# Layer-3 storage order, load times, finish order and table load in a four-layer kernel

## The chip, the cores and the metric

One NeuronCore of a Trainium2 chip. The metric is device time in microseconds of one execution; the number shown is the median of three runs.

## What is computed

x has 4 sequences of 256 tokens by 256 channels, 1024 tokens. Four layers are added in turn, x = x + ffn_l(cond_l(...)). Each cond_l is a gated two-sided recurrence over the tokens (a "ratio" of two scans) times a sigmoid of x. The feed-forward parts differ:

- layer 0: ternary weights and int8 activations (256 to 1024 to 256);
- layer 1: a mixture of 8 experts, two per token, exact gelu, f32 weights;
- layer 2: int weights with zero point 128, silu(gate) * up, 256 to 704 (stored as 768) to 256;
- layer 3: layer norm, then two linear maps in MXINT8, 256 to 1024 to 256, with a tanh gelu between. Both operands are quantised in blocks of 32 along the contraction:

```python
def mx_quant(x):                 # blocks of 32 along the last axis
    amax = max(abs(block)); scale = 2 ** (floor(log2(amax)) - 6)
    return clip(round(block / scale), -128, 127) * scale
h = mx_layernorm(x, ln_w, ln_b)
h = mx_gelu(bf16(mx_quant(h) @ mx_quant(W1).T + b1))
out = bf16(x + bf16(mx_quant(h) @ mx_quant(W2).T + b2))
```

The order in which the 1024 inner units of layer 3 stand in memory is free, as long as blocks of 32 stay blocks.

## The kernel before

It is written with five hand-ordered instruction streams (SP, POOL = GpSimd, ACT = ScalarE, DVE = VectorE, PE = TensorE) and semaphores; every order below is written out in the code, and each engine works in order.

**Expert loop (L950 DVE, L1250 PE, L570 ACT).** 24 tiles of 128 token slots. In iteration j PE multiplies tile j by its expert's first matrix (L1259), transposes tile j+1 (x_transpose), multiplies tile j-1 by the second matrix (down_tile, L1243), and transposes tile j's hidden values (L1269). DVE adds the bias (L954), does one piece of side work, copies the output of tile j-1 to yo (L226) and half of hT (L978). ACT does gelu (L581), the other half of hT (L587), the copy of the transposed input (copy_xT, L544), the store of yo and the load of xg three tiles ahead. The side work of DVE: the recurrences of layers 2 and 3 in j < 18 (ratio_step; the last ratio is ready at j = 17); the absolute maxima and clipping of the third layer's weights W1 and W2 in j = 19 to 22 (L964, block_scales L937, L967); the conversion of layer 2's integers in j = 23 (L971, L973). ACT issues the loads: load_w3 at j = 18 behind the last ratio (L553), load_rows at 19 (L566), load_l2 at 20 (L561).

**The inner index.** Inner unit h of layer 3 is 32n + j (n the block). Before, it is stored j-major, 32 blocks to a run. So W1 is loaded in four transfers of permuted rows of 1 KB (L555 to L557), b1 in three transfers of single 4-byte elements by SP (L283), W2's quantised form is written turned by POOL (L402 to L404), and the gelu's quantiser takes its maxima over a view whose inner step is 32 elements (L1065); the products with `inverse` and `unit` (L1075, L1080) repeat a run of 32. The bias rows br sit in partitions 0, 64 and 96 of brf, which POOL clears (L386) and splits into three bf16 parts (L388 to L392); the matmul with `pick` (L1346, L1364) adds them. POOL then quantises W1 and W2 (L399 to L404) and PE transposes them behind the loop (transpose_w3, L233), into banks 0 to 3.

**Between the layers.** PE transposes the ratio of layer 3 into banks 3 to 6 (L1276), then adds the experts' bias part for all tokens into banks 0 to 3 (L1283). DVE adds all four banks to x (L993), then runs combine(0), scale_y2T(0), combine(1) (L1090). combine(p) needs the two gathered expert rows of each token of group p, which POOL fetches by indirect DMA (L414), after the gather of cb (L410).

**Groups (L1093 DVE, L1368 PE, L646 ACT).** Layers 2 and 3 run over G = 4 groups of two tiles, in rounds p = 0 to 5: layer 2 of group p beside layer 3 of group p-1 and p-2. Layer 2: x_to_channels (L1296), sigmoid_l2, scale_y2T, six chunks of gate_up_l2 (L1309, silu_l2 L613, gate_l2 L1012) in three banks that rotate by the list `turns`, down_l2 (L1318), add_l2 (L1018). Layer 3: norm_stats, norm_apply, norm_quant, norm_to_channels (L1332), copy_hqT (L618), up_l3 (L1344, L1346), gelu_l3 (L625 twice, L630), gelu_scales (L1065 to L1069), gelu_quant (L1075 to L1080), turn_l3 (L1355), copy_q3T, down_l3 (L1363), copy_ob (L643), finish_tile (L1086, L1087), and SP's store. On DVE a round runs: add_l2, finish_tile, norm_stats, scale_y2T, gates with the norm's steps between them, finish_tile, gelu_scales and gelu_quant of tile 2p-3, gelu_scales and gelu_quant of tile 2p-2, combine(p+2).

## Time and profile before

| | us |
|---|---|
| median of 3 runs | 616.39 (616.28 to 618.4) |
| profiled execution, own time | 620.55 |
| its span | 618.5 |
| PE busy / DVE busy | 376.3 / 429.3 |
| ACT busy / POOL busy | 229.8 / 180.1 |

The granted clock of TensorE was 0.83 of full speed on average. A timeline row gives start, duration, engine, line, operation, and in brackets how long the engine was idle before it and who released it. "PEld" is a weight load, "ACTq" and "SPq" are DMA issues. A row may merge neighbours ("x16"); its duration is then their stretch.

### The profile page before, as it was taken

The numbers are of one execution on the slowest core, as the hardware profiler recorded it, in microseconds if no ns is written. First come the engines' busy times: TensorE is split into PE (matmuls) and PEld (weight loads), VectorE is DVE, ScalarE is ACT, GpSimd is POOL, SyncE is SP. The second block draws the span as 40 slices with busy tenths as digits, with TensorE's granted clock in tenths as the row PEclk, the third lists the DMA queues.
The fourth block names the chain that finished last, engine by engine and source line by source line (L and its number), as shares of the span: only waits on it lengthen the run. The fifth ranks groups of instructions, "written<-read, shape, count | busy, mean of one in ns | idle before, by whom it ended". The sixth has DMA issues, their size and how long they took to land.

```text
span 618.5 us, 5497 instructions
## 1 busy us (share of the span) xinstructions
PE 376.3 (61%) x1680; PEld 259.5 (42%) x1680; DVE 429.3 (69%) x615; ACT 229.8 (37%) x333; POOL 180.1 (29%) x116
## 2 busy tenths in 40 slices
PE   0000260435454204999999999946948699798552
PEld 0000220213243102667767766624646577676421
DVE  5999759798774886856966867326673346789873
ACT  4626651447756121222222222202202236365451
POOL 4600213953003483440360330036364600000000
PEclk9999856575678555899999999987977699799875
DMA  8900000000027521281061561995001300000000
GB/s 296 333 0 0 1 0 0 1 0 0 0 98 246 210 76 47 91 302 38 27 205 35 196 212 34 45 153 179 17 10 51 93 1 0 1 10 17 10 17 17
DMA packets 34673, 47.46 MB, mean 77 GB/s; under 512 B 5699, under 2 KB 28758, under 8 KB 34646
## 3 DMA queue, kind: packets, MB, share of 16 engines
q1 hardware_dynamic: 23046, 31.76, 15.1%
q10 hardware_dynamic: 10032, 11.14, 8.2%
q0 software_dynamic: 1568, 4.20, 2.1%
q8 instruction: 15, 0.25, 0.2%
q14 instruction: 12, 0.10, 0.1%
HBM read 37.67 MB, written 9.44 MB: 76 GB/s over the span
## 4 chain that ended last, share of the span: by engine, by line
PE 42%; DVE 19%; issue 19%; POOL 7%; ACT 6%; DMA 6%; ACTq 1%; SPq 0%; POOLq 0%; DVEq 0%
PE bank L1259 12%; PE bank L1243 11%; PE bank L1309 6%; DMA ekv<-in_w3b 4%; POOL slot_rows L375 3%; PE bank L1269 3%; PE bank L1163 3%; DVE scr L723 2%; DVE small L1065 1%; PE bank L1283 1%; DMA small<-in_s_gu 1%; DVE scr L973 1%; POOL ekv L326 1%; PE bank L1318 1%; POOL scr L334 1%
## 5 line engine op out<-in xcount | busy, mean ns | idle before, releaser
L1243 PE MATMUL bank<-big,yT 128*128 x384 | 91.6, 394 | 16.8 <-ACT yT L587 16.8
L1259 PE MATMUL bank<-big,ygT 128*128 x192 | 90.5, 616 | 1.8 <-ACT ygT L544 1.1
L1243 PEld LDWEIGHTS bank<-big,yT 128*128 128x128 f32 x384 | 74.3, 198 | 28.3 <-issue 18.4
L954 DVE TENSOR_TENSOR yT<-bank,big 128x512 f32<-128x512 f32 x48 | 32.8, 689 | 42.7 <-PE bank L1259 42.7
L351 POOL TENSOR_TENSOR small<-small 128x2 f32<-128x2 f32 (+1 forms) x9 | 9.1, 1009 | 173.4 <-DVE small L1032 88.0
L587 ACT ACTIVATE yT<-bank 128x512 f32<-128x512 f32 x24 | 14.3, 597 | 109.3 <-DVE yo L226 82.7
L1259 PEld LDWEIGHTS bank<-big,ygT 128*128 128x128 f32 x192 | 36.0, 198 | 39.3 <-issue 39.3
L1309 PE MATMUL bank<-yT,scr 128*128 128x256 f32 x192 | 46.7, 403 | 0.0
L1163 PE MATMUL bank<-big 128*128 128x512 bf16 x64 | 22.6, 515 | 30.9 <-DVE big L828 29.9
L1309 PEld LDWEIGHTS bank<-yT,scr 128*128 128x128 f32 x192 | 38.6, 205 | 5.5
L340 POOL TENSOR_TENSOR scr<-scr 128x1024 f32<-128x1024 f32 x5 | 15.5, 3108 | 87.1 <-DVE scr L723 87.1
L544 ACT ACTIVATE ygT<-bank 128x256 f32<-128x256 f32 x24 | 9.2, 384 | 66.9 <-PE bank L1234 61.2
L1142 PE MATMUL bank<-identf,yT 128*128 128x128 f32 x16 | 3.6, 417 | 41.8 <-DVE yT L791 41.8
L581 ACT ACTIVATE yT<-yT 128x512 f32<-128x512 f32 x48 | 27.7, 622 | 3.1 <-DVE yT L954 3.1
L226 DVE COPY yo<-bank 128x256 f32<-128x256 f32 x24 | 10.0, 418 | 26.6 <-PE bank L1243 22.2
L331 POOL TENSOR_TENSOR g<-g,ek 128x1024 f32<-128x1024 f32 x8 | 19.0, 2372 | 28.7 <-ACT g L448 28.6
L1269 PE MATMUL bank<-identf,yT 128*128 128x128 f32 x192 | 25.6, 278 | 2.4 <-ACT yT L581 2.4
L1234 PE MATMUL bank<-identf,xg 128*128 128x128 f32 x48 | 9.7, 287 | 27.4 <-DMA xg<-slot_rows 27.4
L1163 PEld LDWEIGHTS bank<-big 128*128 128x128 bf16 x64 | 7.1, 120 | 44.2 <-DVE big L828 34.0
L1269 PEld LDWEIGHTS bank<-identf,yT 128*128 128x128 f32 x192 | 22.9, 143 | 5.0 <-ACT yT L581 2.7
L375 POOL DMA_INDIRECT slot_rows<-y,posi x16 | 20.6, 1289 | 12.6 <-DVE posi L907 8.0
L1234 PEld LDWEIGHTS bank<-identf,xg 128*128 128x128 f32 x48 | 6.8, 147 | 40.6 <-issue 33.8
(284 smaller groups left out, 891.7 us busy)
## 6 DMA issues: line engine op xcount, KB each, us to landing
big<-in_moe_w SPq DMA_DIRECT2D x16, 1024.0 KB, 7.0
big<-in_moe_b SPq DMA_DIRECT2D x8, 512.0 KB, 8.8
slot_rows<-zeros SPq DMA_DIRECT2D x1, 3072.0 KB, 12.9
xg<-slot_rows ACTq DMA_DIRECT2D x24, 128.0 KB, 2.1
slot_outputs<-yo ACTq DMA_DIRECT2D x24, 128.0 KB, 1.7
v<-in_kT SPq DMA_DIRECT2D x1, 1024.0 KB, 5.0
yT<-in_xT SPq DMA_DIRECT2D x1, 1024.0 KB, 8.1
big<-in_gateT SPq DMA_DIRECT2D x1, 1024.0 KB, 10.1
```

The source lines that it names most:

```text
L331: link(gp.tensor_tensor(g[:, l, k], g[:, l, k], ek[:, k], ALU.subtract))
L340: link(gp.tensor_tensor(den[n % 2], den[n % 2], db[:], ALU.add))
L375: gp.indirect_dma_start(out=XG, out_offset=bass.IndirectOffsetOnAxis(ap=posi[:, k, i:i + 1], axis=0), in_=y1[:, i], in_offset=None).then_i ...
L581: sc.activation(h1[:, h * 512:(h + 1) * 512], h1[:, h * 512:(h + 1) * 512], ACT.Gelu).then_inc(s["h1_ready"], 1)
L587: sc.activation(hT[:, 0:4], ps[5][:].rearrange("p (c t) -> p c t", c=4), ACT.Copy).then_inc(s["hT_copy"], 1)
L954: ve.tensor_tensor(h1[:, h * 512:(h + 1) * 512], ps[1 + 2 * (j % 2) + h][:], big[:, bass.ds(at + (B1_AT + h * 512), 512)], ALU.add).then_i ...
L1163: ins = te.matmul(ps[6 + m - 2 * (n % 2)][:], q0T[:, k, tile_cols(i)], wgu_t[:, m, k, h * 512:(h + 1) * 512], start=(k == 0), stop=(k == K ...
L1234: ins = te.transpose(ps[0][:, k * P:(k + 1) * P], xg[:, j % 3, k * P:(k + 1) * P], identf[:])
L1243: ins = te.matmul(ps[7][:, 0:C], hT[:, c], big[:, bass.ds(at + (W2_AT + c * C), C)], start=(c == 0), stop=(c == IC - 1))
L1259: ins = te.matmul(ps[1 + 2 * (j % 2) + h][:], ygT[:, j % 2, k], big[:, bass.ds(at + (k * HI + h * 512), 512)], start=(k == 0), stop=(k == ...
L1269: ins = te.transpose(ps[5 + h][:, (c % 4) * P:(c % 4 + 1) * P], h1[:, c * P:(c + 1) * P], identf[:])
L1309: ins = te.matmul(bank_of((p, c))[:, m * 256:(m + 1) * 256], qgu[:, m, k, c * P:(c + 1) * P], yT[:, k, 256 * p:256 * (p + 1)], start=(k == ...
```

## The change

- **Inner index.** Unit h = 8i + r (i in 0 to 127, r in 0 to 7) is now stored r-major: eight runs of 128. A block of 32 is then 4 neighbours in each of the 8 runs. W1 is loaded in one transfer with 8 KB in a row per partition; W2 is quantised in plain order and read by transpose_w3 with a step of 8 elements; b1 is read by L1346 with a step of 8. The maxima go over two axes with runs of 4; `inverse` and `unit` are written four times each, 128 wide.
- **Bias rows.** No POOL clear and no SP transfers: both rows are broadcast to all partitions with the other rows by ACT (5 transfers), at j = 18, behind the last ratio.
- **Load times.** load_w3 at j = 15 (waiting for the scans and the products with v), load_rows at 18, load_l2 at 19.
- **Entry.** The experts' bias goes to banks 3, 4, 5 and 7; each combine(p) adds its own. Group 0's chunks come ahead of group 1's transposes, sigmoid and scaling, on PE, ACT and DVE.
- **Finishes.** finish_tile of tiles 5, 6 and 7 stands behind gelu_quant of tile 7.
- **Table.** The gelu table load stands ahead of copy_hqT.

```diff
-        turns = ["x0", "x1"]
+        turns = ["x0"]
         for p in range(G):
-            turns += [(p, c) for c in range(HC2)] + ([f"x{p + 2}"] if p + 2 < G else [])
+            turns += [(p, c) for c in range(HC2)]
+            if p == 0:
+                turns += ["x1", "x2"]
+            elif p + 2 < G:
+                turns += [f"x{p + 2}"]
+        bias_banks = (3, 4, 5, 7)
...
-            pe.wait_ge(s["w3q"], 2 * KC)
+            pe.wait_ge(s["w3q"], 2)
...
-                        src = w3q[:, 1, k * H3 + c * P:k * H3 + (c + 1) * P]
+                        src = w3q[:, 1, k * H3:(k + 1) * H3].rearrange("p (i r) -> p r i", r=HC3)[:, c]
...
-            sp.wait_ge(s["br_zero"], 1)
-            for row in (0, 64, 96):
-                sp.dma_start(brf[row:row + 1, 0:H3].rearrange("p (j n) -> p j n", n=32),
-                             A["b3a"].rearrange("(n j) -> j n", n=32).unsqueeze(0),
-                             allow_slow_non_contiguous=True).then_inc(s["ld_bias"], 16)
-                sp.dma_start(brf[row:row + 1, H3:H3 + C], A["b3b"].unsqueeze(0)).then_inc(s["ld_bias"], 16)
...
-            pool.wait_ge(s["ratio_ready"], 2 * L)
-            gp.memset(brf, 0.0).then_inc(s["br_zero"], 1)
-            pool.wait_ge(s["ld_bias"], 16 * 6)
+            pool.wait_ge(s["ld_l3rows"], 16 * 5)
...
-                for k in range(KC):
-                    n = slice(32 * k, 32 * (k + 1))
-                    turned = w3q[:, m, k * H3:(k + 1) * H3].rearrange("p (j n) -> p n j", n=32) if m else \
-                        w3q[:, m, k * H3:(k + 1) * H3].rearrange("p (n j) -> p n j", j=32)
-                    gp.tensor_tensor(turned, w3v[:, n], half[:, n], ALU.subtract).then_inc(s["w3q"], 1)
+                gp.tensor_tensor(w3q[:, m].rearrange("p (n j) -> p n j", j=32), w3v, half, ALU.subtract).then_inc(s["w3q"], 1)
...
             def load_w3():
-                act.wait_ge(s["ratio_ready"], 2 * L)
-                rows = A["w3a"].rearrange("(n c j) k -> j n c k", n=32, c=HC3)
-                for j in range(4):
-                    act.dma_start(w3nat[0][32 * j:32 * (j + 1)].rearrange("p (c k) -> p c k", c=HC3), rows[j]).then_inc(s["ld_w3"], 16)
+                act.wait_ge(s["scanned"], 2 * len(POOL_SUMS))
+                act.wait_ge(s["gv_ready"], 2 * L)
+                act.dma_start(w3nat[0].rearrange("p (c k) -> p c k", c=HC3),
+                              A["w3a"].rearrange("(p c) k -> p c k", c=HC3)).then_inc(s["ld_w3"], 16)
...
             def load_rows():
-                for dst, n in ((sdrow, "s_down"), (lnw, "ln_w"), (lnb, "ln_b")):
+                act.wait_ge(s["ratio_ready"], 2 * L)
+                for dst, n in ((sdrow, "s_down"), (lnw, "ln_w"), (lnb, "ln_b"), (brf[:, 0:H3], "b3a"), (brf[:, H3:H3 + C], "b3b")):
...
             for j in range(TILES):
-                if j == 18:
+                if j == 15:
                     load_w3()
+                elif j == 18:
+                    load_rows()
                 elif j == 19:
-                    load_rows()
-                elif j == 20:
                     load_l2()
...
-                if p + 1 < G:
+                if p >= 1 and p + 1 < G:
                     sigmoid_l2(p + 1)
...
+                if p == 0:
+                    sigmoid_l2(1)
                 if 1 <= p <= G:
+                    sc.preload_act_table(ACT.Gelu_apprx_tanh)
                     copy_hqT(p - 1)
                     gelu_l3(2 * p - 2)
...
-            for p in range(G):
+            def combine(p):
                 dve.wait_ge(s["bias_ready"], p + 1)
-                ve.tensor_tensor(pair(x, p), pair(x, p), ps[p][:], ALU.add).then_inc(s["bias_added"], 1)
-
-            def combine(p):
+                ve.tensor_tensor(pair(x, p), pair(x, p), ps[bias_banks[p]][:], ALU.add).then_inc(s["bias_added"], 1)
...
-            unit = ex3[:, 1].bitcast(BF16)[:, 0:32]
-            inverse = ex3[:, 2].bitcast(BF16)[:, 0:32]
+            unit = ex3[:, 1:3].rearrange("p m n -> p (m n)").bitcast(BF16)[:, 0:P]
+            inverse = ex3[:, 1:3].rearrange("p m n -> p (m n)").bitcast(BF16)[:, P:2 * P]
...
-                link(ve.tensor_reduce(top3, gl3[i % 2].rearrange("p (j n) -> p n j", n=32), AX.X, ALU.max, apply_absolute_value=True))
+                link(ve.tensor_reduce(top3, gl3[i % 2].rearrange("p (r n q) -> p n r q", r=HC3, q=4), AX.XY, ALU.max, apply_absolute_value=True))
...
             combine(0)
             scale_y2T(0)
-            combine(1)
             for p in range(G + 2):
                 if 1 <= p <= G:
                     add_l2(p - 1)
-                if p >= 3:
+                if 3 <= p <= G:
                     finish_tile(2 * p - 5)
...
-                if p + 1 < G:
+                if p >= 1 and p + 1 < G:
                     scale_y2T(p + 1)
                 if p < G:
                     gate_l2(p, 0)
+                if p == 0:
+                    combine(1)
...
+                if 2 <= p <= G:
+                    finish_tile(2 * p - 4)
                 if p >= 2:
-                    finish_tile(2 * p - 4)
                     gelu_scales(2 * p - 3)
...
+                if p == 0:
+                    scale_y2T(1)
                 if p + 2 < G:
                     combine(p + 2)
-            finish_tile(T - 1)
+            for i in range(T - 3, T):
+                finish_tile(i)
...
+            pe.wait_ge(s["r3_copy"], 2)
+            pe.wait_ge(s["r3_copy2"], 2)
...
-                    te.matmul(ps[4 + h][:], pick[:], br[:, h * 512:(h + 1) * 512], start=False, stop=True).then_inc(s["u3_ready"], 1)
+                    te.matmul(ps[4 + h][:], pick[:], br[:, 0:H3].rearrange("p (i r) -> p r i", r=HC3)[:, 4 * h:4 * h + 4], start=False, stop=True).then_inc(s["u3_ready"], 1)
...
-                if p + 1 < G:
+                if p >= 1 and p + 1 < G:
                     x_to_channels(p + 1)
...
+                if p == 0:
+                    x_to_channels(1)
                 if p < G:
                     down_l2(p, 0)
```

## Rows read from the trace of the kernel before

**Rows 1.** The timeline around expert tile 19 (start us, us, engine, line, what; idle before)

```profile
403.91 1.04 PE L1269 MATMUL bank<-identf,yT 128*128 128x128 f32 x8
...
413.97 2.29 DVE L964 TENSOR_REDUCE small<-ek 128x64 f32<-128x2048 f32 x1 [12.73 <-DMA ekv<-in_w3b]
...
427.71 1.04 PE L1269 MATMUL bank<-identf,yT 128*128 128x128 f32 x8
...
435.69 1.04 PE L1269 MATMUL bank<-identf,yT 128*128 128x128 f32 x8
```

**Rows 2.** The timeline where VectorE works beside GpSimd

```profile
417.11 2.65 DVE L941 TENSOR_SCALAR small<-small 128x64 f32<-128x64 f32 x1
...
447.00 10.83 POOL L404 TENSOR_TENSOR v<-ekv,tcmp 128x1024 bf16<-128x1024 f32 x2
...
448.90 4.43 DVE L971 TENSOR_SCALAR scr<-scr 128x3072 f32<-128x3072 int32 x1
...
453.25 5.69 DVE L973 SCALAR_TENSOR_TENSOR scr<-scr 128x1536 f32<-128x1536 int32 x1
...
460.42 6.74 PE L1243 MATMUL bank<-big,yT 128*128 x16 [7.94 <-ACT yT L587]
```

**Rows 3.** The timeline of groups 1 to 3

```profile
516.91 0.59 ACT L618 ACTIVATE big<-bank 128x512 bf16<-128x512 bf16 x1
...
519.68 1.28 ACT L630 ACT_TABLE_LOAD   x1
...
529.08 1.11 PE L1296 MATMUL bank<-identf,x 128*128 128x128 f32 x4 [3.58 <-DVE x L1000]
...
529.98 3.62 PE L1309 MATMUL bank<-yT,scr 128*128 128x256 f32 x8
...
547.12 2.86 PE L1318 MATMUL bank<-scr,big 128*128 128x256 f32 x12 [0.23 <-DVE big L1012]
...
570.71 2.86 PE L1318 MATMUL bank<-scr,big 128*128 128x256 f32 x12 [0.71 <-DVE big L1012]
```

**Rows 4.** The timeline of the tail, tiles 6 and 7

```profile
595.26 1.88 DVE L1065 TENSOR_REDUCE small<-big 128x32 f32<-128x1024 bf16 x1 [1.40 <-ACT big L630]
...
605.87 1.86 DVE L1065 TENSOR_REDUCE small<-big 128x32 f32<-128x1024 bf16 x1
...
610.15 0.69 DVE L1080 TENSOR_TENSOR big<-big,small 128x1024 bf16<-128x1024 bf16 x1
...
616.00 0.42 DVE L1087 TENSOR_TENSOR x<-x,big 128x256 f32<-128x256 f32 x1
```

**Rows 5.** The DMA issues (KB each, us from issue to landing)

```profile
ekv<-in_w3b ACTq DMA_DIRECT2D x1, 1024.0 KB, 22.6
...
cb<-slot_outputs,crow_i POOLq DMA_INDIRECT x1, 2.2
```

**Rows 6.** Groups by form from 380 us on (busy us, mean ns of one)

```profile
L1065 DVE TENSOR_REDUCE small<-big 128x32 f32<-128x1024 bf16 x8 | 15.0, 1877 | 7.0 <-ACT big L630 6.8
...
L404 POOL TENSOR_TENSOR v<-ekv,tcmp 128x1024 bf16<-128x1024 f32 x2 | 10.8, 5612 | 0.1
...
L404 POOL TENSOR_TENSOR v<-ek,small 128x1024 bf16<-128x1024 f32 x2 | 3.8, 1912 | 0.1
...
L1045 DVE TENSOR_REDUCE small<-big 128x16 f32<-128x512 bf16 x4 | 2.7, 679 | 0.0
```

**Rows 7.** The chain that ended last, group 1 and 2 (start us, us, what)

```profile
518.16 0.22 PE bank L1346
...
537.47 6.92 PE bank L1309 x32
```

**Rows 8.** The timeline at the entry of layer 2

```profile
472.56 6.37 PE L1283 MATMUL bank<-cb,big 16*128 16x256 f32 x16 [1.87 <-DMA cb<-slot_outputs,crow_i]
...
475.33 0.96 POOL L414 DMA_INDIRECT g<-slot_outputs,posi  x1 [0.30 <-issue]
...
486.88 12.30 PE L1309 MATMUL bank<-yT,scr 128*128 128x256 f32 x48
```

More of the change, by code:

```diff
@@ L961, in _ @@
                     if j == 19:
-                        dve.wait_ge(s["ld_w3"], 80)
+                        dve.wait_ge(s["ld_w3"], 32)
                     if j % 2:
@@ L1064, in gelu_scales @@
                 top3 = ex3[:, 0, 0:32]
[L1065 removed]
+                link(ve.tensor_reduce(top3, gl3[i % 2].rearrange("p (r n q) -> p n r q", r=HC3, q=4), AX.XY, ALU.max, apply_absolute_value=True))
                 link(ve.tensor_scalar(top3.bitcast(I32), top3.bitcast(I32), 0x7F800000, None, ALU.bitwise_and))
                 link(ve.tensor_scalar(top3, top3, 2.0 ** -120, None, ALU.max))
[L1068 to L1069 removed]
+                bits = top3.bitcast(I32).unsqueeze(2).to_broadcast(by_block)
+                ve.tensor_scalar(inverse.bitcast(I16).rearrange("p (n q) -> p n q", q=4), bits, -1.0 / 65536, 260.0 * 128, ALU.mult, ALU.add)
+                link(ve.tensor_scalar(unit.bitcast(I16).rearrange("p (n q) -> p n q", q=4), bits, 1.0 / 65536, -6.0 * 128, ALU.mult, ALU.add))
             def gelu_quant(i):
[L1072 removed]
                 t = m3[:, 0:512].bitcast(BF16)
[L1074 to L1075 removed]
+                t3 = t.rearrange("p (r i) -> p r i", r=HC3)
+                g3 = gl3[i % 2].rearrange("p (r i) -> p r i", r=HC3)
+                link(ve.tensor_tensor(t3, g3, inverse.unsqueeze(1).to_broadcast([P, HC3, P]), ALU.mult))
                 link(ve.tensor_scalar(t, t, MAGIC, MAGIC, ALU.add, ALU.subtract))
@@ L1079, in gelu_quant @@
                     dve.wait_ge(s["q3_tr"], i - 1)
-                ve.tensor_tensor(q3[i % 2].rearrange("p (j n) -> p j n", n=32), t.rearrange("p (j n) -> p j n", n=32),
-                                 unit.unsqueeze(1).to_broadcast(by_block), ALU.mult).then_inc(s["q3_ready"], 1)
+                ve.tensor_tensor(q3[i % 2].rearrange("p (r i) -> p r i", r=HC3), t3,
+                                 unit.unsqueeze(1).to_broadcast([P, HC3, P]), ALU.mult).then_inc(s["q3_ready"], 1)
                 dve.wait_ge(s["q3_ready"], i + 1)
@@ L1282, in _ @@
             for i in range(T):
-                ins = te.matmul(ps[i // 2][:, (i % 2) * C:(i % 2 + 1) * C], gcT[:, tile_cols(i)], cb[:], start=True, stop=True)
+                ins = te.matmul(ps[bias_banks[i // 2]][:, (i % 2) * C:(i % 2 + 1) * C], gcT[:, tile_cols(i)], cb[:], start=True, stop=True)
                 if i % 2:
@@ L1288, in x_to_channels @@
                 pe.wait_ge(s["l1_done"], 2 * p + 2)
-                if p == 0:
-                    pe.wait_ge(s["bias_added"], G)
                 if freed(f"x{p}"):
@@ L1326, in norm_to_channels @@
                     pe.wait_ge(s["q3T_ready"], 2 * p - 1)
-                else:
-                    pe.wait_ge(s["r3_copy"], 2)
-                    pe.wait_ge(s["r3_copy2"], 2)
                 for k in range(KC):
@@ L1361, in down_l3 @@
                     pe.wait_ge(s["ob_ready"], i)
+                else:
+                    pe.wait_ge(s["bias_added"], G)
                 for c in range(HC3):
```

10 lines of the change are left out of this document (3 added, 7 removed).

## The prediction, made before the run

> **What bounds the kernel now.** I read the page first, for the stages, then the timeline from 388 us on, because the change touches nothing before expert tile 15 and the first stall that it can reach is at tile 19. The expert loop is paced by TensorE at 7.98 us a tile: the transposes of two neighbouring tiles start at 427.71 and 435.69 [rows 1]. One interval is 23.80 us, from 403.91 to 427.71. In it VectorE's first reduction of the third-layer weights sits 12.73 us on the load of ekv until 413.97 [rows 1], and its copy of hT, for which TensorE waits, is queued behind it. In the last tile VectorE converts weights beside GpSimd: L971 and L973 together hold it from 448.90 to 458.94, and TensorE's L1243 starts at 460.42 after 7.94 us of idleness [rows 2]. The third and fourth layers then run as groups of two tiles. In group 1 TensorE is idle 3.58 us before L1296, for combine(3) on VectorE; in groups 2 and 3 it runs nearly without a gap, with 0.23 and 0.71 us at L1318 [rows 3]. From 595 us on the kernel is one serial chain of gelu, quantiser, transposes, product and finish, tile after tile [rows 4].
>
> **The weight load (gain 14.8).** It is issued at tile 15 instead of 18, three tiles or 24 us sooner, at about 365. Even with the 22.6 us to landing that it took [rows 5] it is there at 388, and tile 19 wants it near 400; its two transfers go past ACT's xg load, which is not wanted for nearly two tiles, and its new waits (scans and the products with v) end around tile 13. SP's six bias loads go. So 23.80 - 7.98 = 15.8 us come back. Against it: the five row broadcasts are issued at tile 18 (a few us of ScalarE's time, where it waits for TensorE's transposes of xg anyway), GpSimd's bias work (five operations) starts when they land, and VectorE's small operations of tile 19 meet it. L941, on 64 columns, took 2.65 us when GpSimd was busy [rows 2], and 64 columns are no work for that. Four such, with the hT copy behind them, cost 0 (bias work over in time) to 3; I take 1.0, as the copy has a few us of slack behind TensorE's L1259.
>
> **Tile 23 (gain 6.5).** GpSimd's last writes of w3q were turned, 5612 ns per 1024 columns against 1912 for plain ones [rows 6]. L971 ends some 1.6 us after the first turned write, L973 just after the second, at 457.83: they wait for GpSimd. With one plain write of 2 x 1.91 from 447.00 GpSimd ends at 450.8; L971 is done at 452.4, and L973 (1536 columns at L1045's 1.04 ns [rows 6] and a fixed part of 0.15: 1.75) at 454.2. Before, that was 458.94: 4.8, with the rounding of the copies behind it 5.0. Then the clock: L1243's 16 matmuls took 6.74 us here after the idle time and 3.46 is the price of 16 like ones at pace [rows 7]. With some 2.9 us of idleness (452.5 to 455.4) it may stay up or not, 0 to 3.1; I take 1.5. The turned third-layer weight is instead read by TensorE in steps of 16 bytes: 16 transposes, priced below, 0 to 2.5 (a quarter of 0.65 each), taken at 0.5 because the gather of cb hides the rest.
>
> **Entry of layer 2 (gain 5.4).** The first chunk of L1309 starts at 486.88, behind group 1's transposes, which wait for combine(1) [rows 8]. Bias banks 3, 4, 5 and 7 free VectorE of three bias additions ahead of combine(0). What limits combine(0) then is the gather of tile 1, issued at 475.33, landing 2.2 later by the cb gather's time [rows 5]: 477.5, and 1.0 for its two operations, 478.5. TensorE's bias products end at 478.9 [rows 8], so they are the next limit. Transposes (1.1, as at L1296 [rows 3]), sigmoid and scaling (each the size of L1045's 0.68) follow: first chunk at 481.5. combine(1), 2.7 us with its addition (0.68), goes between the first two gates, while a slow first chunk of 3.5 us leaves VectorE little else; group 1's transposes go into the gap before L1318, and its scaling and combine(2) are done within L1318's 24 products. I cost these at nothing; without that cover they would cost up to 2.7.
>
> **Groups 1 to 3 (cost 4.0, less 1.1).** ScalarE works in order, so the gelu load, 1.28 us, now starts after the group's last silu, and copy_hqT behind it. Before, that copy followed the silu at once (516.91) and the load came later, at 519.68 [rows 3]. For the gelu nothing changes: the load only moves ahead on the same chain. For TensorE, which waits for hqT, 1.28 us are new. Next, L1346 reads br with a step of 8 bf16. No row has TensorE reading so. Contiguous it takes 0.22 us in the chain [rows 7] at the high clock, the lower end; the upper end is VectorE's L1065, which at a 64-byte step needs (1877 - 150) / 1024 = 1.69 ns a column against 1.04 for L1045 [rows 6], so 0.86 us. I take a doubling, 0.43, nearer to TensorE's own row: plus 0.43 a tile on the gelu's chain, 0.86 a group on TensorE. The Trainium skill, "SBUF — State Buffer" (Door 1: the DMA port swizzle, the note on cachelines), says that full bandwidth needs two hits on each 16-byte line, and also that eight bf16 can be stridden for free. This step is exactly on that border: by the second half the price is nil and the sum 3 us better, by the first it is a penalty of unstated size. No run here shows it. On VectorE each quantiser gains: L1065 in runs of four costs about 1.22 us like L1045's rate (0.65 less), two small writes of 128 instead of 32 columns 0.1 more each: 0.45 net. Group 1: gelu 0.43 late, quantiser 0.45 faster, bias addition 0.68 more: 0.7 late for combine(3). Group 2 is bound by TensorE: 1.28 less 0.23 of idleness at L1318, plus 0.86: 1.9. Group 3: 1.28 less 0.71, plus 0.86: 1.4 [rows 3]. Together 4.0; with free reading 1.9, at the upper end 8.4. Group 1's gap of 3.58 us cost clock: eight matmuls of L1309 took 3.62 us behind it; 32 of them took 6.92 later, 1.73 for eight [rows 3, 7]. The gap shrinks to about 2; that gives back 0 to 2.2, taken 1.1.
>
> **Tail (gain 7.4).** Here ScalarE is idle before hqT, so the load is hidden: gelu(6), for which L1065 of tile 6 waited 1.40 us, comes 1.3 sooner, 0.4 less for L1346: L1065 at 594.3 instead of 595.26 [rows 4]. Scales and quantiser take 4.98 us (605.87 to L1080's end, 610.85), less 0.45: done at 598.85. L1065 of tile 7 follows at once instead of at 605.87, where it stood behind finish_tile(6) and so behind tile 6's product: done at 603.4 against 610.85. finish_tile(5), needed by the last copy_ob, and (6) run during tile 7's transposes and product, which take the old 5.57 us (610.85 to 616.42): end 609.0 instead of 616.42.
>
> **Sum.** 14.8 + 6.5 - 0.5 + 5.4 - 4.0 + 1.1 + 7.4 = 30.7 us. Against the profiled execution's 620.55 (span 618.5) this is 589.9; the runs' median is 616.39, 4.2 lower, so I forecast 585.7, told as 586.
>
> **Rivals.** (a) The 16-byte step costs TensorE nothing: 3.0 better, 582.7. For it: the step is a quarter of L1065's, the only slow read that the trace has. Against it: that row is over 1.6 times the contiguous price a column. Chance 0.22. (b) It costs the upper end, 0.65 us a matmul; 14 of 16 lie in the path, the 16 transposes count a quarter each, so 18 x 0.65 less 2.0 of slack, 9.7 instead of 3.0: 592.4. Chance 0.15. (c) The gelu load is hidden in groups 1 to 3 too, if the last silu leaves earlier than norm_to_channels ends: 3.6 better, 582. Against it: the copy at 516.91 follows its silu without a gap [rows 3]. Chance 0.06. (d) The gathers land late once the bias additions no longer cover them: half the entry's gain is lost, 588.5. Chance 0.05. (e) Slower than before: the strided read is priced as GpSimd's turned write, 5612 / 1024 = 5.5 ns a column [rows 6], 2.87 us a matmul. Then 18 x 2.66 less 2.0 is 45.9, against 33.7 of gains without that cost: 628.6. It decides from 2.2 us a matmul on, ten times the plain price. Against it: those writes were slowed by VectorE's work beside them. Chance 0.02. (f) The wait at tile 19 does not go, because the transfer's slowness is in the load itself: even then it lands ten us ahead of the need. Chance under 0.01. The forecast keeps 0.50.
>
> **Numbers.** The range 579.5 to 595 holds (a) to (d) with the unknown costs (clock 0 to 5.3, GpSimd beside VectorE 0 to 3, the strided price) and leaves out their coincidences and (e). Half a per cent, 3 us, is about what a measurement can tell from no change. Faster needs a gain of only 3 of 30.7: 0.97; within 0.5% 0.01; slower 0.02.
>
> **What would show it.** Right: transposes L1269 every 8 us through tiles 18 to 21; L973 under 2.5 us; the first chunk of L1309 before L1296 of group 1, about 5 us after group 0's; in groups 1 to 3 the table load ahead of L618, with TensorE idle over 2 us there; L1346 about 0.2 us longer; L1065 at 1.2; last L1065 about 4.6 us after the one before. Wrong: a VectorE wait on a load at tile 19, combine(0) waiting for gathers beyond 479, L1346 unchanged or 0.65 longer, or a last quantiser waiting for its gelu.

## The result, and the profile after

The changed kernel takes **597.83 us** (median of 4 runs, 595.41 to 600.27); the kernel before took 617.11 us beside it (4 runs, 616.28 to 618.4). The ratio is 0.969, with a 95% interval from 0.963 to 0.974. It is faster by 3.1%, some 19 us. The forecast was 586.0 us, with a range from 579.5 to 595: the sign was right, the gain was foreseen some 60% too large (30.7 us for 19.3), and the time lies above the range. The profiled execution took 595.98 us, with a span of 594.2.

A table by stage shows where the difference is. Its borders are starts of instructions that can be found in either timeline: the transposes of tiles 18 and 23 (L1269, now L1271), the four VectorE additions that end the groups (now L1013) and the last finish (now L1084). Line numbers have moved: L1243 is now L1245, L1309 L1311, L1318 L1320, L1346 L1345, L1065 L1061, L1087 L1084, L971 and L973 L968 and L970.

| Stage | before, us | after, us | gained | forecast |
|---|---|---|---|---|
| start to tile 18 | 395.25 | 396.65 | -1.4 | 0 |
| tile 18 to tile 23 (weight load) | 56.19 | 40.57 | 15.6 | 14.8 |
| tile 23 to the end of group 0 (tile 23, entry) | 54.30 | 43.28 | 11.0 | 11.4 |
| groups 1 to 3 | 72.39 | 81.02 | -8.6 | -2.9 |
| tail | 37.87 | 30.13 | 7.7 | 7.4 |

The forecast of each stage is the sum of its terms. Three of the stages came within 1 us of it. Groups 1 to 3 lost three times what was forecast.

The timeline of the changed kernel around tile 19 (start us, us, engine, line, what; idle before and what ended it), where the kernel before had the 12.73 us of [rows 1]:

```profile
401.88 2.28 DVE L961 TENSOR_REDUCE small<-ek 128x64 f32<-128x2048 f32 x1
...
404.42 2.50 DVE L938 TENSOR_SCALAR small<-small 128x64 f32<-128x64 f32 x1
...
404.63 1.04 PE L1271 MATMUL bank<-identf,yT 128*128 128x128 f32 x8
...
406.95 1.28 DVE L939 TENSOR_SCALAR small<-small 128x64 f32<-128x64 f32 x1
408.14 0.18 DVE L940 TENSOR_SCALAR small<-small 128x64 f32<-128x64 f32 x1
...
413.49 1.04 PE L1271 MATMUL bank<-identf,yT 128*128 128x128 f32 x8
...
418.72 2.28 DVE L961 TENSOR_REDUCE tcmp<-ekv 128x64 f32<-128x2048 f32 x1
```

And GpSimd's part of the same timeline:

```profile
404.24 2.62 POOL L388 TENSOR_TENSOR scr<-scr 32x1280 f32<-32x1280 f32 x1
406.93 1.25 POOL L389 CAST scr<-scr 32x1280 bf16<-32x1280 f32 x1
```

Neither reduction shows a wait on a load. What stands there is the meeting that the forecast had costed at 1.0. L938 begins at 404.42 and ends at 406.92, where L388 ends (404.24 + 2.62 = 406.86); L939 ends at 408.23, where L389 does (408.18). An operation of 64 columns, 0.2 us elsewhere, lasts until GpSimd's is over. From tile 19's transposes to tile 20's it is 8.86 us (404.63 to 413.49) instead of 7.98: 0.88 us. In e12 below only one of the two small operations was held so, and the interval stayed 7.98. The stage gained 15.6 and not 14.9 because the interval before tile 19, which was 8.66 us, is 7.98 too.

Tile 23 went as costed, and so did the entry up to the first chunk:

```profile
432.79 3.64 POOL L397 TENSOR_TENSOR v<-ekv,tcmp 128x2048 bf16<-128x2048 f32 x1
...
434.69 3.36 DVE L968 TENSOR_SCALAR scr<-scr 128x3072 f32<-128x3072 int32 x1
...
437.97 1.75 DVE L970 SCALAR_TENSOR_TENSOR scr<-scr 128x1536 f32<-128x1536 int32 x1
...
441.19 5.40 PE L1245 MATMUL bank<-big,yT 128*128 x16 [2.93 <-ACT yT L581]
...
446.43 2.05 PE L248 MATMUL bank<-identb,v 128*128 128x128 bf16 x32
...
452.11 4.14 PE L1287 MATMUL bank<-cb,big 16*128 16x256 f32 x16 [1.88 <-DMA cb<-slot_outputs,crow_i]
...
458.65 1.11 PE L1298 MATMUL bank<-identf,x 128*128 128x128 f32 x4 [2.40 <-DVE x L995]
...
461.27 2.05 PE L1311 MATMUL bank<-yT,scr 128*128 128x256 f32 x4 [1.50 <-DVE yT L1000]
```

GpSimd writes w3q in one plain operation of 3.64 us where two turned ones took 10.83 [rows 2]; VectorE's L970 takes the forecast 1.75 us; TensorE's last product waits 2.93 us, not 7.94. From the bias products to the first chunk it is 9.16 us (452.11 to 461.27), where it was 14.32 (472.56 to 486.88, [rows 8]): 5.2 for the forecast 5.4.

Now a group. The timeline of group 0's third-layer part in the changed kernel:

```profile
491.79 1.28 ACT L661 ACT_TABLE_LOAD   x1
493.09 0.60 ACT L612 ACTIVATE big<-bank 128x512 bf16<-128x512 bf16 x1
493.97 0.38 PE L1343 MATMUL bank<-w3T,big 128*128 128x512 bf16 x1 [2.48 <-ACT big L612]
494.18 1.06 PE L1345 MATMUL bank<-scr,pick 128*128 128x512 bf16 x1
495.06 0.61 PE L1343 MATMUL bank<-w3T,big 128*128 128x512 bf16 x2
495.51 1.06 PE L1345 MATMUL bank<-scr,pick 128*128 128x512 bf16 x1
496.39 4.32 PE L1320 MATMUL bank<-scr,big 128*128 128x256 f32 x12
...
503.19 2.77 PE L1320 MATMUL bank<-scr,big 128*128 128x256 f32 x12
```

The same place by windows of time (us, busy time of PE, PEld, DVE, ACT and POOL, then the granted clock, DMA share, GB/s):

```profile
491.50:494.00 2.50, 0.03 (x1) 0.15 (x3) 0.79 (x2) 2.15 (x3) 0.00 (x0) 1.00 0.00 0
494.00:496.40 2.40, 2.40 (x6) 0.57 (x6) 0.00 (x0) 0.60 (x1) 0.00 (x0) 0.95 0.00 0
496.40:500.60 4.20, 4.20 (x14) 3.32 (x13) 2.14 (x6) 1.66 (x2) 0.00 (x0) 0.62 0.00 0
500.60:503.20 2.60, 2.60 (x8) 0.65 (x7) 2.46 (x5) 0.60 (x1) 0.00 (x0) 1.00 0.00 0
```

And one such matmul in the chain that ended last (start us, us, what), beside the 0.22 of [rows 7]:

```profile
494.35 0.90 PE bank L1345
```

Three things are to be seen. TensorE is idle 2.48 us for the table load and the copy behind it, in each of the three groups. (The record of the first product behind it is missing here, in e1 and in e4; where it stands, in e5 to e7, e9 and e11, the idle time is 2.25. With no load ahead it is 1.05 counted the first way (e2) and 0.83 the second (e12).) The bias matmul L1345 costs 0.90 us, 0.68 more than before; the forecast took 0.22 more. And the next twelve products take 4.32 us where twelve like them take 2.77 a moment later: the clock went down to 0.62 of full speed on average (so it was at 1.2 GHz most of that time) and came back. In the next two groups these twelve took 4.28 and 3.93, so that the slow products cost 4.3 us in all. The forecast had the clock give 1.1 us back in the groups, in the chunks at the start of group 2. It did so there: the eight matmuls that took 3.62 us [rows 3] take 1.89. What it took behind the table load had no term.

The tail, in the changed kernel's timeline (VectorE):

```profile
578.27 1.22 DVE L1061 TENSOR_REDUCE small<-big 128x32 f32<-128x1024 bf16 x1 [1.58 <-ACT big L624]
...
583.08 1.22 DVE L1061 TENSOR_REDUCE small<-big 128x32 f32<-128x1024 bf16 x1 [0.38 <-ACT big L624]
...
591.65 0.42 DVE L1084 TENSOR_TENSOR x<-x,big 128x256 f32<-128x256 f32 x1
```

The last two quantisers start 4.81 us apart (10.61 before, [rows 4]) and the reductions take 1.22 us, as forecast.

### The profile page after: what moved, and what is told of

Read it like the earlier page. It is cut to its first block, busy times and chain, and to the rows that moved or that the text cites. A ratio compares the mean times of both kernels' runs of the same rounds, so it can differ in the third digit from the quotient of the medians.

```text
span 594.2 us, 5483 instructions
## 1 busy us (share of the span) xinstructions
PE 381.8 (64%) x1673; PEld 259.0 (44%) x1680; DVE 418.8 (70%) x615; ACT 231.4 (39%) x333; POOL 172.5 (29%) x113
## 4 chain that ended last, share of the span: by engine, by line
PE 48%; issue 18%; DVE 17%; POOL 8%; ACT 6%; DMA 3%; ACTq 0%; SPq 0%; POOLq 0%; DVEq 0%
PE bank L1261 13%; PE bank L1245 13%; PE bank L1311 5%; POOL slot_rows L374 3%; PE bank L1271 3%; PE bank L1320 3%; PE bank L1165 3%; DVE scr L720 2%; PE bank L1345 2%; DMA small<-in_s_gu 1%; POOL ekv L325 1%; POOL scr L333 1%; PE bank L1343 1%; DVE small L800 1%; PE bank L1236 1%
## 5 line engine op out<-in xcount | busy, mean ns | idle before, releaser
L1245 PE MATMUL bank<-big,yT 128*128 x384 | 88.9, 385 | 4.6 <-ACT yT L581 4.6
L1245 PEld LDWEIGHTS bank<-big,yT 128*128 128x128 f32 x384 | 72.3, 193 | 15.2 <-issue 6.1
L1311 PE MATMUL bank<-yT,scr 128*128 128x256 f32 x192 | 45.0, 393 | 1.5 <-DVE yT L1000 1.5
L1311 PEld LDWEIGHTS bank<-yT,scr 128*128 128x128 f32 x192 | 37.3, 198 | 7.0 <-issue 1.9
L1320 PE MATMUL bank<-scr,big 128*128 128x256 f32 x96 | 26.3, 433 | 0.6 <-DVE big L1007 0.6
L1271 PE MATMUL bank<-identf,yT 128*128 128x128 f32 x192 | 25.0, 273 | 2.4 <-ACT yT L575 2.4
L1320 PEld LDWEIGHTS bank<-scr,big 128*128 128x128 f32 x96 | 21.3, 223 | 9.1 <-issue 4.2
L1271 PEld LDWEIGHTS bank<-identf,yT 128*128 128x128 f32 x192 | 22.4, 141 | 5.1 <-ACT yT L575 2.7
```

What stands on the lines that cost most here:

```text
L1245: ins = te.matmul(ps[7][:, 0:C], hT[:, c], big[:, bass.ds(at + (W2_AT + c * C), C)], start=(c == 0), stop=(c == IC - 1))
L1271: ins = te.transpose(ps[5 + h][:, (c % 4) * P:(c % 4 + 1) * P], h1[:, c * P:(c + 1) * P], identf[:])
L1311: ins = te.matmul(bank_of((p, c))[:, m * 256:(m + 1) * 256], qgu[:, m, k, c * P:(c + 1) * P], yT[:, k, 256 * p:256 * (p + 1)], start=(k == ...
L1320: ins = te.matmul(ps[3][:, t * C:(t + 1) * C], h2T[p % 2][:, c, t * P:(t + 1) * P], qd[:, c], start=(c == 0), stop=(c == HC2 - 1))
```

## The experiments

The theory behind the first runs: the strided read of the bias row by TensorE costs 0.68 us a matmul, and together with the idle time in front of it also the clock. The rival: the table load alone makes the loss, through the 2.48 us. The changed kernel was timed again beside them, since its own executions lie 5 us apart.

**e4, the changed kernel again.** No edit.

> The changed kernel again, unaltered. Its four executions lay at 595.4, 596.0, 599.7 and 600.3. Theory C (two levels some 4 us apart by chance of the clock in each execution): again both levels. Otherwise one level within 1 us.

It took 595.98 us (594.39 to 598.57, 6 runs; ratio 0.962, interval 0.958 to 0.967). Groups 1 to 3 took 81.4 us in its profile. Its twelve products behind the idle time took 2.77, 4.44 and 4.04 us in the three groups; the slow ones cost 3.6 us here. This is the run against which e1 to e3 are read; the kernel before took 619.09 us (11 runs) beside them.

**e1, the bias row turned once by ScalarE, so that TensorE reads it in a row.**

```diff
+            sc.activation(br2.rearrange("p (r i) -> p r i", r=HC3), br[:, 0:H3].rearrange("p (i r) -> p r i", r=HC3),
+                          ACT.Copy).then_inc(s["br_turned"], 1)
...
-                    te.matmul(ps[4 + h][:], pick[:], br[:, 0:H3].rearrange("p (i r) -> p r i", r=HC3)[:, 4 * h:4 * h + 4], start=False, stop=True).then_inc(s["u3_ready"], 1)
+                    te.matmul(ps[4 + h][:], pick[:], br2[:, h * 512:(h + 1) * 512], start=False, stop=True).then_inc(s["u3_ready"], 1)
```

> The changed kernel, but ScalarE turns the bias row once (ahead of layer 2, where it is idle) so that L1345's counterpart reads 512 neighbours instead of steps of 16 bytes. Theory A (the step makes TensorE's matmul 0.88 us instead of 0.22, and some 12 of 16 lie in the path): the matmul is back at 0.22 in the chain and the kernel 6 to 9 us faster than the changed one, 589 to 592. Theory B (the groups lost their time to the exposed table load and the clock behind it; the slow matmul hides in that): under 2 us faster. Theory C (the missing microseconds are a spread between executions): no difference.

586.62 us (585.09 to 588.07), 9.4 us below e4. Groups 1 to 3 took 70.9 us, 10.6 below e4. The timeline of its first group:

```profile
496.92 0.38 PE L1348 MATMUL bank<-w3T,big 128*128 128x512 bf16 x1 [2.48 <-ACT big L617]
497.13 0.38 PE L1350 MATMUL bank<-scr,pick 128*128 128x512 bf16 x1
...
498.00 2.75 PE L1325 MATMUL bank<-scr,big 128*128 128x256 f32 x12
```

The idle time is the same 2.48 us, and the products behind it run at full speed in all three groups. So without the strided read the loss in the groups is gone, and in this run the idle time alone did not bring the clock down. That is theory A, with a little more than its 6 to 9 us.

**e2, no table load ahead of copy_hqT.**

```diff
-                    sc.preload_act_table(ACT.Gelu_apprx_tanh)
```

> The changed kernel without the early load of the gelu table; the strided read stays. Theory A: 1.28 us come back on TensorE in groups 2 and 3 and little in group 1, 1.3 are lost in the tail: 0 to 3 us faster. Theory B: TensorE's wait before up_l3 falls from 2.48 to about 1.2 us in three groups, the clock stays up (1.4 us each), 1.3 is lost in the tail: 4 to 7 us faster, 591 to 594. Theory C: no difference.

593.93 us (592.71 to 597.28), 2.0 below e4, which is not clear of the scatter (ratio 0.961, interval 0.955 to 0.967; e4's is 0.962). In the profiles groups 1 to 3 took 74.7 us, 6.7 below e4, but the tail grew from 30.2 to 32.1; e4's profiled execution was one of its slower ones (597.69). The timeline of its second group:

```profile
520.75 0.38 PE L1342 MATMUL bank<-w3T,big 128*128 128x512 bf16 x1 [1.05 <-ACT big L612]
520.97 1.06 PE L1344 MATMUL bank<-scr,pick 128*128 128x512 bf16 x1
...
523.17 2.77 PE L1319 MATMUL bank<-scr,big 128*128 128x256 f32 x12
```

The read is as slow, the idle time 1.05, and the clock holds in all three groups. The median fits theory A, the profile theory B.

**e3, turned as in e1, and the table loaded ahead only behind the last group**, where ScalarE is idle.

```diff
-                    sc.preload_act_table(ACT.Gelu_apprx_tanh)
+                    if p == G:
+                        sc.preload_act_table(ACT.Gelu_apprx_tanh)
```

> The changed kernel with the turned bias row, and the early table load only in the last round, where ScalarE is idle before hqT. If A and B both hold their costs add: 11 to 15 us faster than the changed kernel, 583 to 587, the best of these. If they hide each other, no more than the better of the two single runs by 2 us. Theory C: no difference.

586.06 us (584.05 to 588.18), ratio 0.945 (0.940 to 0.950): 0.6 below e1, which is within the scatter. The two savings did not add to 11 to 15 us; it is no faster than the better of the two. Groups 70.1 us, tail 29.9.

**e12, turned and without any table load ahead**, the fourth corner beside e4, e1 and e2.

> The changed kernel with the bias row turned once and with no table load ahead at all: the fourth corner beside the changed kernel, e1 (turned, loaded ahead) and e2 (strided, not loaded ahead). Theory (the two parts cost more together than apart): groups 1 to 3 take 70 to 71 us as in e1, so that the load ahead costs under 1 us without the strided read where it cost 6.7 us of groups with it; behind the last group the load costs 2 us as in e2, so the time is 1 to 2.5 us above e3 (586.1), near 587 to 588.5. Rival (their costs simply add): groups of 64 to 65 us, and a time near 582 to 584.

589.57 us (587.77 to 590.35), timed beside a kernel before of 616.14 us; the forecast of the time was 587 to 588.5. The groups took 70.3 us, the tail 31.2. The four corners, groups 1 to 3 in us:

| | loaded ahead | not loaded ahead |
|---|---|---|
| strided read | 81.4 (e4) | 74.7 (e2) |
| turned row | 70.9 (e1) | 70.3 (e12) |

As they stand, the costs do not add: the load ahead costs 6.7 us beside the strided read and 0.6 without it, the strided read 10.5 beside the load and 4.4 without. But the clock differs from corner to corner. In e4 the slow products cost 3.6 us, in e1 and e2 none. In e12 TensorE waits 3.78 us for combine(3) in the second group, where e1 shows 2.5, and the eight matmuls behind it take 3.58 us for 1.89: 1.7 us. An estimate without these: 77.9 (e4), 74.7 (e2), 70.9 (e1) and 68.7 us (e12). Then the load ahead costs 3.2 us beside the strided read and 2.2 without it, and the strided read 7.0 and 6.0: the two add within 1 us. What did not add is the clock.

**e6, the strided matmul replaced by four contiguous ones**, so that TensorE is held as long (4 x 0.22 us) but reads in a row. The bias is added four times and in another order.

```diff
-                    te.matmul(ps[4 + h][:], pick[:], br[:, 0:H3].rearrange("p (i r) -> p r i", r=HC3)[:, 4 * h:4 * h + 4], start=False, stop=True).then_inc(s["u3_ready"], 1)
+                    for n in range(4):
+                        ins = te.matmul(ps[4 + h][:], pick[:], br[:, h * 512:(h + 1) * 512], start=False, stop=(n == 3))
+                    ins.then_inc(s["u3_ready"], 1)
```

> The changed kernel with each strided bias matmul of the second up product replaced by four contiguous ones into the same bank, about the same TensorE time (4 x 0.22 for 0.90 us); this adds the bias four times over and in the unturned order, so that part of the computation is changed. It tells whether the clock falls behind the table load because TensorE is late by so much, or because it reads slowly. Theory A (a slow read passes few columns a microsecond, and with the 2.48-us idle that brings the granted clock down): the clock stays up, the first products of groups 1 to 3 behind the idle stay near 2.75 us rather than 4.3, and the time is 4 to 6 us below the changed kernel. Theory B (only the time counts, or the idle): the clock falls as before and the time is within 1.5 us of the changed kernel.

599.03 us (598.56 to 601.16), 1.2 us above e7, which was timed beside it. The timeline of its second group:

```profile
524.21 0.60 PE L1343 MATMUL bank<-w3T,big 128*128 128x512 bf16 x2 [2.25 <-ACT big L612]
524.65 1.03 PE L1346 MATMUL bank<-scr,pick 128*128 128x512 bf16 x4
...
526.81 2.75 PE L1320 MATMUL bank<-scr,big 128*128 128x256 f32 x12
```

And in its third group, behind the same idle time:

```profile
550.94 1.90 PE L1346 MATMUL bank<-scr,pick 128*128 128x512 bf16 x4
...
553.48 1.46 PE L1346 MATMUL bank<-scr,pick 128*128 128x512 bf16 x4
```

The twelve products took 2.75 us in all three groups. But in the third the clock had fallen earlier: the two sets of four took 1.90 and 1.46 us for 1.03, the products between them 1.06 for 0.59, and the granted clock is 0.66 from 550 to 555 us; this costs 1.7 us. So the part of theory A on the clock held in two groups of three, and a slow read isn't needed for the clock to fall. Its time did not hold; the time is theory B's, within 1.5 us. The groups came to 79.0 us, 8.2 above e1 and 2.0 below the changed kernel. Less the 1.7 they are 6.5 above e1; the changed kernel's 81.0 less its 4.3 are 5.9 above e1, and e4's 81.4 less 3.6 are 7.0. So of the changed kernel's 10 us some 6 are time on TensorE (of the 8.2 that twelve times 0.68 give) and some 4 the clock. The 2.0 us do not show in the time: tile 18 was reached 2.0 us later than in e7's profile, before anything that was edited, and the tail took 0.9 more.

**e11, four steps in one kernel.** The row is turned as in e1 but the bias matmuls read the unturned one, in steps of 2, 4, 16 and 8 elements for two tiles each; the bias then stands in other orders.

```diff
+                    r = (2, 4, 16, 8)[i // 2]
+                    te.matmul(ps[4 + h][:], pick[:], br[:, 0:H3].rearrange("p (i r) -> p r i", r=r)[:, h * r // 2:(h + 1) * r // 2], start=False, stop=True).then_inc(s["u3_ready"], 1)
```

> The kernel with the bias row turned once by ScalarE (e1), but the bias matmuls of the second up product read the unturned row in steps of 2 elements (4 bytes) for tiles 0 and 1, of 4 (8 bytes) for tiles 2 and 3, of 16 (32 bytes) for tiles 4 and 5, of 8 (16 bytes) for tiles 6 and 7; the bias then stands in other orders, so that part of the computation is changed. It gives the price of a step by itself. Theory A (the cost grows with the bytes that a column is away from the next, up to a line): about 0.22 us a matmul at 2 elements, 0.44 at 4, 0.90 at 8 and at 16. Theory B (any step over one element costs the whole): 0.90 at each. Theory C (it goes on with the step): 0.90 at 8 and 1.8 at 16.

595.35 us (595.22 to 595.88). In its timeline one matmul each of tile 1 (step 2), tile 2 (4), tile 4 (16) and tile 6 (8):

```profile
502.70 0.39 PE L1351 MATMUL bank<-scr,pick 128*128 128x512 bf16 x1
...
523.27 0.61 PE L1351 MATMUL bank<-scr,pick 128*128 128x512 bf16 x1
...
549.58 1.08 PE L1351 MATMUL bank<-scr,pick 128*128 128x512 bf16 x1
...
572.53 1.08 PE L1351 MATMUL bank<-scr,pick 128*128 128x512 bf16 x1
```

A contiguous one shows 0.38 in e1's timeline and 0.22 in the chain; the 0.16 between is the part that overlaps the next. Less that, a step of 4 bytes costs 0.23 us, nothing more than none; 8 bytes 0.45; 32 bytes 0.92, all three at full clock. The row at 16 bytes is from the tail, where the granted clock is 0.50 (571 to 575 us): also 0.92. At full clock it is the 0.90 of the changed kernel, so the read at 16 bytes takes as long at either level of the clock. That is theory A: the price is that of none up to 4 bytes, then doubles with the distance up to 16 bytes and stays. The Trainium skill, "SBUF — State Buffer" (Door 1, the note on cachelines), has both that eight bf16 can be stridden for free and that full bandwidth needs two hits on a 16-byte line. For TensorE's moving operand this trace agrees with neither: at 16 bytes the read takes four times as long, and at 8 bytes, with two hits on a line, still twice (0.45 for 0.22 us). For a source that is loaded as weights the step is nearly free: the 32 transposes L248, half of them strided, took 2.05 us, and 1.95 before.

**e7, the weight load back at tile 18**, in its new form.

```diff
-                if j == 15:
+                if j == 18:
                     load_w3()
-                elif j == 18:
                     load_rows()
```

> The changed kernel with the load of the third layer's weights issued at tile 18 again, where the kernel before had it, but in its new contiguous form. Theory (the old wait of 12.7 us at tile 19 came from what was loaded, 4-byte pieces in the queues, and not from when): the loads land in 6 to 9 us of their issue, nothing or at most 2 us is waited, and the time is within 2 us of the changed kernel. Rival (it is the place that counts: these loads are slow beside the gathers of tiles 18 and 19): they take some 16 to 22 us again, and the time is 10 to 13 us above the changed kernel.

597.8 us (597.49 to 598.53), the changed kernel's own time. The loads, in e7's list of DMA issues (KB each, median us from issue to landing), against the 22.6 us of [rows 5]:

```profile
ek<-in_w3a ACTq DMA_DIRECT2D x1, 1024.0 KB, 5.2
ekv<-in_w3b ACTq DMA_DIRECT2D x1, 1024.0 KB, 8.7
```

The three tiles of earlier issue bring nothing once the load is fast: tile 18 to tile 23 takes 40.6 us either way. What the change had removed was the slowness.

**e8, the kernel before with b3a loaded as plain rows**, where it was fetched turned, in 3 x 1024 pieces of 4 bytes; the bias then stands in another order. The weights' loads keep their old form and place.

```diff
-                sp.dma_start(brf[row:row + 1, 0:H3].rearrange("p (j n) -> p j n", n=32),
-                             A["b3a"].rearrange("(n j) -> j n", n=32).unsqueeze(0),
-                             allow_slow_non_contiguous=True).then_inc(s["ld_bias"], 16)
+                sp.dma_start(brf[row:row + 1, 0:H3], A["b3a"].unsqueeze(0)).then_inc(s["ld_bias"], 16)
```

> The kernel before with the bias b3a loaded as plain rows in place of the turned ones of 3072 pieces of 4 bytes; so the bias stands in another order, and that part of the computation is changed. Theory (the 4-byte pieces are what holds the queues): the load of the weights lands in under 12 us, the wait of VectorE at tile 19 goes from 12.7 us to under 3, and the time is 9 to 14 us below the kernel before. Rival (the weights' own transfers with their inner index of 32 rows are the slow part): the wait stays above 9 us and the time within 3 us of the kernel before.

605.48 us (601.4 to 605.72) against 619.08 beside it: 13.6 us from three transfers of 4 KB. Its DMA issues and its timeline at tile 19:

```profile
ek<-in_w3a ACTq DMA_DIRECT2D x4, 256.0 KB, 4.8
ekv<-in_w3b ACTq DMA_DIRECT2D x1, 1024.0 KB, 8.1
```

```profile
402.52 2.28 DVE L962 TENSOR_REDUCE small<-ek 128x64 f32<-128x2048 f32 x1
...
418.48 2.28 DVE L962 TENSOR_REDUCE tcmp<-ekv 128x64 f32<-128x2048 f32 x1
```

No wait is left, and every tile of that stretch took 7.98 us or less. The 4-byte pieces on SP's queue held up the megabytes on ACT's; the layout of the weights' own transfer, which is the old one here, did not make the wait.

**e5, the finishes of tiles 5 and 6 back in their old places.**

```diff
-                if 3 <= p <= G:
+                if p >= 3:
                     finish_tile(2 * p - 5)
...
-                if 2 <= p <= G:
+                if p >= 2:
                     finish_tile(2 * p - 4)
...
-            for i in range(T - 3, T):
-                finish_tile(i)
+            finish_tile(T - 1)
```

> The changed kernel with the finishes of tiles 5 and 6 back in their old places ahead of the last quantisers. Theory (their VectorE time lies on the path to the last quantiser): the tail, from the last add_l2 to the last finish, goes from 30.1 us back to some 35 to 38 us, and the time is 5 to 7 us above the changed kernel (two finishes of some 3.5 us each ahead of the last quantiser, less what of them is then missing behind it). Rival (the shorter tail comes from the shorter quantiser alone, its reductions 1220 for 1877 ns, and the order is indifferent): at most 1.5 us above the changed kernel.

604.72 us (603.57 to 607.03), 6.9 above e7. The tail took 35.0 us, 4.9 more, and the last two reductions were 8.68 us apart:

```profile
580.98 1.22 DVE L1061 TENSOR_REDUCE small<-big 128x32 f32<-128x1024 bf16 x1 [1.57 <-ACT big L624]
...
589.20 0.42 DVE L1084 TENSOR_TENSOR x<-x,big 128x256 f32<-128x256 f32 x1
...
589.66 1.22 DVE L1061 TENSOR_REDUCE small<-big 128x32 f32<-128x1024 bf16 x1
```

The last quantiser stands behind the finish of tile 6 again. The order of the finishes is worth 5 of the tail's 7.7 us. The two profiled executions lie 5.9 us apart: 4.9 in the tail, 1.9 in the stretch from tile 23 to group 0 and 0.4 ahead of tile 18, which this edit does not touch, less 1.1 in the groups.

**e9, group 1's transposes, combine and turns back ahead of group 0's chunks.** The diff is the entry's part of the change, undone: `turns = ["x0", "x1"]`, and sigmoid_l2(1), combine(1), scale_y2T(1) and x_to_channels(1) in their old places.

> The changed kernel with group 1's transposes, its combine and its turns back in their old places ahead of group 0's chunks. Theory (they lie on VectorE's and TensorE's path to group 0's first chunk): that chunk starts 3 to 5 us later after the last expert product, part of it is given back before the first add_l2, and the time is 2 to 4 us above the changed kernel. Rival (the gathers or the layer's input hold the entry, whatever the order): within 1 us of the changed kernel.

599.3 us (598.34 to 599.95), ratio 0.970 (0.963 to 0.977): 1.5 above the changed kernel's 597.83, 3.3 above e4, in another session; by the ratios to the kernel before, 0.970 against 0.969 and 0.962, the time is not clear of the scatter, and it is neither the theory's 2 to 4 nor the rival's under 1. The first chunk is. From the bias products to the first chunk it took 12.61 us for the changed kernel's 9.16, so 3.45 later. In its timeline combine(1) and the transposes stand in front of the chunk:

```profile
460.07 0.68 DVE L984 TENSOR_TENSOR x<-x,bank 128x512 f32<-128x512 f32 x1
...
462.97 1.09 PE L1289 MATMUL bank<-identf,x 128*128 128x128 f32 x4 [4.17 <-issue]
463.85 2.77 PE L1302 MATMUL bank<-yT,scr 128*128 128x256 f32 x6
```

**e10, the kernel before, profiled once more.**

> The kernel before, unaltered, profiled a second time. It shows how far one execution stands from another in the stages that the change does not touch: if the profiled execution of the sum was an ordinary one, its stages come within 0.5 us of the first profile's; if the clock differs from execution to execution, some stage differs by 1 us or more, with another granted clock beside it.

618.71 us, span 616.7, beside timed runs of the kernel before from 614.98 to 623.1. The second case held: the stretch from tile 23 to the end of group 0 took 52.6 us (54.3 in the first profile), groups 1 to 3 71.3 (72.4), all else within 0.5. In that first stretch the sixteen products of tile 23 took 5.26 us here and 6.74 there, and in the changed kernel's variants anything from 3.71 to 6.74: the clock behind the same idle time differs from execution to execution.

## Why the prediction was wrong

**Weight load: size right, reason wrong.** Forecast 14.8, measured 15.6 (16.1 against e10). The prediction took the 22.6 us to landing as given and counted on the earlier issue. e7 shows that the earlier issue is worth nothing once the pieces are gone, e8 that the removed 4-byte pieces are worth it all. By the prediction's own working (issued at about 365, landed 22.6 later at 388, wanted near 400) the earlier issue would have sufficed with the pieces in place; no run shows that. Rival (f), "the transfer's slowness is in the load itself", looked at the wrong load. The meeting with GpSimd was taken at 1.0 and measured 0.88, and tile 18's 0.68 came on top.

**Tile 23 and entry: about right in the pair of profiles, helped by the clock.** VectorE's part of tile 23 came as worked out (TensorE's last product began 3.97 us behind the tile's transposes, for 8.98 before: 5.0), and so did the first chunk. The strided transposes cost 0.1, not 0.5. But in the nine other profiles with the new entry order (e1 to e7, e11, e12) this stage took 44.95 to 47.24 us, for the 43.28 of this one. In e1 to e5 and e11 the products of tile 23 took 6.6 us or more for the 5.40 here; in e5, e6, e7, e11 and e12 TensorE waited 2.0 to 2.4 us more within group 0's chunks, and what made that wait was not followed up. Against 52.6 and 54.3 before, the usual gain is nearer 8 than 11. With the old order of group 1's work (e9) the stage took 47.67, 0.4 to 2.7 us above these nine, so that most of the 3.45 us at the first chunk is given back before group 0 ends.

**Groups 1 to 3: the step that failed.** It read: "I take a doubling, 0.43, nearer to TensorE's own row", and "The gap shrinks to about 2; that gives back 0 to 2.2, taken 1.1". The read costs 0.90, so the price was that of rival (b), "It costs the upper end, 0.65 us a matmul", to which 0.15 had been given. Twelve matmuls at 0.68 more are 8.2 us of TensorE, of which e1, e6 and the corners put some 6 to 7 on the path, where the sum had 2.1 (4.0 less 1.9). The second failure is the clock, which the sum only let give back. It gave the 1.7 us at group 2's first chunks back, but behind the table load, which the forecast itself had put there with TensorE "idle over 2 us", it took 4.3, for which there was no term. Rival (b) alone, at 592.4, is still 5.4 below the measured time.

The table load's own term, 1.28 + 1.05 + 0.57 = 2.9, was about right: without the clock's part it cost 2.2 us with the turned row and 3.2 with the strided one. Of the rest of the change, e1 against the kernel before says this: the first and third of these groups are 0.4 and 0.6 us longer, and the second 2.5 shorter, with a granted clock of 1.00 for 0.89.

**Tail: right.** 7.7 for 7.4. e5 attributes 4.9 of it to the order of the finishes; e2 and e12 show that the table load ahead of the last group saves 1.3 to 1.9.

**The baseline: 6 us of the 12.** Against the profiled 620.55 the sum gave 589.9; the profiled execution of the changed kernel took 595.98, 6.1 more, of which 5.7 are the groups and 1.4 the start up to tile 18, less 0.7 for the other stages and 0.3 outside the two spans. The other half is the step "the runs' median is 616.39, 4.2 lower": the changed kernel's median came out 1.9 above its profiled execution instead. Beside later runs the kernel before had medians of 616.14, 619.08 and 619.09, so the 4.2 taken from three runs and one profiled execution was in good part scatter. A median of three within 0.4% looked firmer than it was.

**What is open.** What brings the clock down in the groups isn't settled. With the table load ahead and the strided read (the changed kernel, e4, e5, e7 and e9) it fell behind the idle time in 14 groups of 15, the twelve products taking 3.2 to 4.4 us. With the load ahead and rows read at full pace it fell in none of e1's three and in one of e6's. In e11 it fell for a step of 2 elements (3.77 us), which costs nothing, and for 4 (4.44), and not for 16 (2.77). With no load ahead (e2, e3, e12) it held there in nine groups of nine, though in e3 and e12 it fell behind the 3.78 us of waiting for combine(3). So the longer idle time goes with it, the slow read makes it more frequent in these runs, neither decides by itself, and chance has a part.

**The better version.** e3 (row turned once, table loaded ahead only where ScalarE is idle) ran at 586.06 us, 9.9 below the changed kernel in the same session and 5.5% below the kernel before. e1 alone gives nearly all of it.

## What to carry to other kernels

When a layout change moves a stride from one engine to another, find what the new reader pays before counting the gain of the old one: here a single copy of 2 us on an idle ScalarE was worth 9 us. A wait on a large load can be made by a tiny one: look for transfers of 4-byte pieces on any queue at the same time before moving the large one. And where a change puts a new idle time in front of TensorE, the sum needs a term for the clock behind it: here the costs of the read and of the load added within 1 us, and the clock's 4 us came on top.

## What the runs showed of the hardware

- TensorE's moving operand (bf16, 512 columns, full clock) takes 0.22 us in the chain contiguous, 0.23 at a step of 4 bytes, 0.45 at 8, 0.90 at 16 and 0.92 at 32 (e1, e11, the changed kernel). At a granted clock of 0.50 the read at 16 bytes took 0.92 too (e11). A source loaded as weights showed 2.05 for 1.95 us over 32 transposes, 16 of them at a step of 16 bytes.
- VectorE's reduction over 1024 bf16 in runs of four takes 1.22 us (1877 ns in steps of 64 bytes, [rows 6]), which is the rate of L1045's contiguous row.
- 3072 pieces of 4 bytes on SP's queue kept transfers of 1 MB on ACT's queue from landing for 22.6 us instead of 8.1.
- A 64-column VectorE operation beside a GpSimd one ends when GpSimd's does: 2.50 us beside L388's 2.62, and 1.28 beside L389's 1.25.
- The same kernel's executions differ by 5 us and more (594.39 to 600.27; the kernel before 614.98 to 625.69), with stages that move by 1 to 2 us from one profile to the next and a different granted clock in them.
